# Order of small steps and column ranges in a fused sparse linear, GELU and FP8 linear kernel

## Chip, cores and metric

The kernel runs on one core of a Trainium2 chip. The metric is the device time of one execution in microseconds (us), lower is better.

## What is computed

x has 4096 rows (8 x 512) of 1024 numbers. Every row is normalised, and two linear layers are applied to the result and added to x:

```
xn   = layernorm(x)                                    # per row, eps 1e-5
attn = (w1^T w2^T) * sparse_mask                        # 1024 x 1024, a band of stripes
y    = gelu(xn attn + b2)
w_q  = fp8_e4m3(weight * 448 / max|weight|)
x_q  = fp8_e5m2(xn * x_scale),  x_scale = 57344 / max|xn|     # one scale for the whole of xn
f    = (x_q w_q^T) / x_scale / w_scale + bias
out  = x + y + f
```

x_scale needs every row of x: no product with x_q can start before the last row is read, squared and searched for its maximum.

## The kernel before

The rows are 32 tiles of 128 (NT = 32), all of them kept in SBUF. Every engine has its program written out by hand in order; engines wait for each other with semaphores.

**First stage.** SyncE loads the weights and the tiles. ScalarE and VectorE make row sums (neg_mean). ScalarE's `square(t)` (L645) makes the squares with their sum (ssq) and counts `squared`; VectorE's `maximum(t)` (L868) takes each row's largest square. TensorE transposes the weights and multiplies w1 with w2; VectorE masks, scales and splits the result into a high and a low half (`attention_high` L906, `attention_low` L910). GpSimd rounds the weights, and makes from ssq, with `deviations(i)` (L534 scaled variance, L537 power -1/2, L540 product), the 1/deviation rs and -mean/deviation nb of the tiles of one entry of `RANGES`.

**The scale of x.** After the last square ScalarE makes var_all from ssq (L733). VectorE, in this order: maximum(31), L973 to L976 (x_rowmax), TensorE spreads it over the partitions, VectorE's L978 (x_sqmax), GpSimd's square root L597 (x_amax), VectorE's x_inv L1027 and x_mul L1028 (x_scale). Then VectorE does sum_parts(1) (L1013), add_b2(0) (L983), four small scalars (L1032 to L1036), add_b2(1), add_gelu(0), add_gelu(1) (L993), add_product(0) (L998), sum_parts(2), seed_f(2) (L1005), add_product(1), seed_f(3), sum_parts(3). GpSimd does `quantiser(0)` and `quantiser(1)` (L547, L548: rs and nb times x_mul, for the tiles of a range; each counts `quant_ready`), `add_bias(0)` and `add_bias(1)` (L578), the scaling of the bias (L605), low(4) and low(5).

**The tiles.** Tile q passes these steps:
- ScalarE `normalise(q)` (L739): x to xn * x_scale. It waits for `quant_ready` by the place of q's range in `RANGES` (`wait_range`, L330). `high(q)` (L745): its rounding to 16 bits.
- GpSimd `low(q)` (L553): what the rounding left.
- SyncE `transpose_parts(q)` (L419): a DMA that transposes both halves into hlT.
- GpSimd `quantise(q)` (L584): the sum of the halves as FP8. For tiles 1 to 3 it is VectorE's sum_parts(q) and ScalarE's quantise(q) (L754).
- TensorE `attention(a)` (L1195) for the pair a, a + 1 into psY and psZ, and `ffn(q)` (L1210) into psT or psF. attention(a) waits from tile 4 on for `seed_y` (L771) of both tiles, with which ScalarE puts b2 into PSUM.
- ScalarE `gelu(q)` (L761, from tile 4 on L765), VectorE `add_gelu(q)`, `add_product(q)`, and SyncE stores.

The engines' loops go over pairs, a = 0, 2, ... 30. TensorE: ffn(a), ffn(a + 1), attention(a + 2); before the loop attention(0), 6 warming matmuls, the spread and 8 more (L1228). ScalarE in turn a: gelu(a), gelu(a + 1) (for a > 0), normalise and high of a + 6, seed_y(a + 2), seed_y(a + 3), normalise and high of a + 7. GpSimd in turn a: low(a + 6), quantise(a + 4), low(a + 7), quantise(a + 5); at a = 2 and a = 8 also deviations and quantiser of the third and the fourth range. What waits on an engine holds up all that stands behind it on that engine.

Of the kernel before, what the change touches and what calls it, by code (L numbers as in the profile page):

```python
# [5 lines left out]
ALU = mybir.AluOpType  # L6
ACT = mybir.ActivationFunctionType
# [10 lines left out]
D = 1024  # L18
# [20 lines left out]
LN_EPS = 1e-5  # L39
AMAX_EPS = 1e-12  # L40
E4M3_MAX, E5M2_MAX = 448.0, 57344.0
XSCALE = 1024.0
# [10 lines left out]
NT = 32  # L53
# [1 line left out]
FIRST = 4  # L55
KEEP_WARM = (6, 8)

RANGES = [(0, 4), (4, 12), (12, 20), (20, 32)]
PAIRS = range(0, NT, 2)
SPREAD_AT = 20  # L60

# [35 lines left out]
def sparse_linear_plus_fp8_linear(  # L97
# [18 lines left out]
    with ExitStack() as ctx:  # L116
        def sb(name, shape, dt):
            return ctx.enter_context(nc.sbuf_tensor(name, shape, dt))
# [4 lines left out]
        def sem(name):  # L123
            return ctx.enter_context(nc.semaphore(name))
# [47 lines left out]
        ssq = sb("ssq", [P, NT], F32)  # L172
# [5 lines left out]
        var_all = sb("var_all", [P, NT], F32)  # L178
# [39 lines left out]
        biases_loaded = sem("biases_loaded")  # L218
# [24 lines left out]
        squared = sem("squared")  # L243
# [4 lines left out]
        var_all_ready = sem("var_all_ready")  # L248
# [81 lines left out]
        def wait_range(eng, signal, q):  # L330

            eng.wait_ge(signal, next(i for i, (lo, hi) in enumerate(RANGES) if q < hi) + 1)

        def wait_xs(eng, q):

            eng.wait_ge(first_xs if q < FIRST else xs_ready, q + 1 if q < FIRST else q - FIRST + 1)

        def wait_hlT(eng, q):

            eng.wait_ge(hlT_loaded[q % HLT_RING], 16 * (q // HLT_RING + 1))  # L340
# [5 lines left out]
        def wait_y(eng, q):  # L346

            for r, n in last_turns(q):
                eng.wait_ge(strip_done[r], n)
# [159 lines left out]
        def _(pool):  # L509
# [21 lines left out]
            def deviations(i):  # L531
                lo, hi = RANGES[i]
                pool.wait_ge(squared, hi)
                nc.gpsimd.tensor_scalar(var_s[:, lo:hi], ssq[:, lo:hi], 1.0 / D / XSCALE ** 2,  # L534
                                        LN_EPS / XSCALE ** 2, ALU.mult, ALU.add).then_inc(var_ready, 1)
                pool.wait_ge(var_ready, i + 1)
                nc.gpsimd.tensor_tensor(rs[:, lo:hi], var_s[:, lo:hi], minus_half[:, 0:hi - lo], ALU.pow)\  # L537
                    .then_inc(rs_ready, 1)
                pool.wait_ge(rs_ready, i + 1)
                nc.gpsimd.tensor_tensor(nb[:, lo:hi], neg_mean[:, lo:hi], rs[:, lo:hi], ALU.mult)\  # L540
                    .then_inc(nb_ready, 1)

            def quantiser(i):

                lo, hi = RANGES[i]
                pool.wait_ge(nb_ready, i + 1)
                nc.gpsimd.tensor_scalar(rs_q[:, lo:hi], rs[:, lo:hi], x_mul, None, ALU.mult)  # L547
                nc.gpsimd.tensor_scalar(nb_q[:, lo:hi], nb[:, lo:hi], x_mul, None, ALU.mult)\  # L548
                    .then_inc(quant_ready, 1)

            def low(q):
                wait_xs(pool, q)
                nc.gpsimd.tensor_tensor(hl[q % HL_RING][:, D:2 * D], xs[:, q % 2, :], hl[q % HL_RING][:, 0:D],  # L553
                                        ALU.subtract).then_inc(xl_ready, 1)

            def parts(q):
                x_q = x_all[:, SLOT[q], :]
                if q < HL_RING:
                    pool.wait_ge(a_step, KB)
                else:  # L560
                    wait_hlT(pool, q - HL_RING)
                nc.gpsimd.tensor_scalar(hl[q % HL_RING][:, 0:D], x_q, rs[:, q:q + 1], nb[:, q:q + 1],
                                        ALU.mult, ALU.add).then_inc(first_high, 1)
                if q == 2:
                    pool.wait_ge(x0_transposed, 1)
                nc.gpsimd.tensor_scalar(xs[:, q % 2, :], x_q, rs[:, q:q + 1], nb[:, q:q + 1],
                                        ALU.mult, ALU.add).then_inc(first_xs, 1)
                pool.wait_ge(first_high, q + 1)
                low(q)
# [4 lines left out]
            def add_bias(q):  # L574

                pool.wait_ge(biases_loaded, 32)
                wait_xs(pool, q)
                nc.gpsimd.tensor_tensor(x_all[:, SLOT[q], :], x_all[:, SLOT[q], :], bias_bc, ALU.add)\  # L578
                    .then_inc(bias_added, 1)

            def quantise(q):
                wait_hlT(pool, q)
                pool.wait_ge(f_done, q - XQ_RING + 1)
                nc.gpsimd.tensor_tensor(quantised(q % XQ_RING), hlT[:, q % HLT_RING, 0:D],  # L584
                                        hlT[:, q % HLT_RING, D:2 * D], ALU.add, saturate=False)\
                    .then_inc(xq_ready, 1)
# [6 lines left out]
            pool.wait_ge(xl_ready, 2)  # L593
            parts(2)
            parts(3)
            pool.wait_ge(x_sqmax, 1)
            nc.gpsimd.tensor_tensor(x_am, x_sq, plus_half[:, :], ALU.pow).then_inc(x_amax, 1)  # L597
            pool.wait_ge(x_scale, 1)
            quantiser(0)
            quantiser(1)  # L600
            add_bias(0)
            add_bias(1)
            pool.wait_ge(f_scale, 1)
            pool.wait_ge(bias_added, 2)
# [2 lines left out]
            def low_scaled(q):  # L607
                pool.wait_ge(xh_ready, q - FIRST + 1)
                low(q)
# [3 lines left out]
            for a in PAIRS:  # L613
                for q in (a, a + 1):
                    if q + AHEAD < NT:
                        low_scaled(q + AHEAD)
                    if q + FIRST < NT:
                        quantise(q + FIRST)
                if a in (2, 8):
                    deviations(2 + a // 8)  # L620
                    quantiser(2 + a // 8)

        @block.scalar
        def _(act):
# [10 lines left out]
            def square(t):  # L635
                wait_x(act, t)
                if KIND[t] == "A":
                    act.wait_ge(mean_a, sums_by("A", t))
                elif KIND[t] == "P":
                    act.wait_ge(mean_p, (sums_by("P", t) + 1) // 2)  # L640
                else:
                    act.wait_ge(mean_v, sums_by("V", t))
                if t >= SQ_RING:
                    act.wait_ge(row_max, t - SQ_RING + 1)
                act.activation(squares[:, t % SQ_RING, :], x_all[:, SLOT[t], :], ACT.Square,  # L645
                               bias=neg_mean[:, t:t + 1], accum_out=ssq[:, t:t + 1]).then_inc(squared, 1)
# [11 lines left out]
            def copy_wq(j):  # L658
# [70 lines left out]
            square(29)  # L729
            square(30)  # L730
            square(31)
            act.wait_ge(squared, NT)
            act.activation(var_all[:, :], ssq[:, :], ACT.Copy, scale=1.0 / D / XSCALE ** 2,  # L733
                           bias=LN_EPS / XSCALE ** 2).then_inc(var_all_ready, 1)

            def normalise(q):
                wait_range(act, quant_ready, q)
# [59 lines left out]
            with when_mask_leaves_band(act):  # L797
# [10 lines left out]
                with act.Fori(0, NT) as t:  # L808
                    act.wait_ge(g_x_loaded, 16 * t + 16)
                    act.activation(g_xs, x_slot, ACT.Identity, scale=rs[:, bass.ds(t, 1)],  # L810
                                   bias=nb[:, bass.ds(t, 1)]).then_inc(g_xs_ready, 1)
# [8 lines left out]
        def _(dve):  # L820
            chain = [0]

            def then(ins):

                chain[0] += 1
                ins.then_inc(v_chain, 1)
                dve.wait_ge(v_chain, chain[0])
# [38 lines left out]
            def maximum(t):  # L866
                dve.wait_ge(squared, t + 1)
                nc.vector.tensor_reduce(maxsq[:, t:t + 1], squares[:, t % SQ_RING, :], AX_X, ALU.max)\  # L868
                    .then_inc(row_max, 1)
# [98 lines left out]
            maximum(28)  # L968
            maximum(29)
            maximum(30)  # L970
            maximum(31)
            dve.wait_ge(var_all_ready, 1)
            then(nc.vector.reciprocal(m2[:, :], var_all[:, :]))  # L973
# [6 lines left out]
            def add_b2(q):  # L980
                wait_y(dve, q)
                y = ps_y[q % 2][:, :]
                nc.vector.scalar_tensor_tensor(out=y, in0=y, scalar=y_mul_first, in1=b2_bc, op0=ALU.mult,  # L983
                                               op1=ALU.add).then_inc(t1_ready, 1)
# [22 lines left out]
            def sum_parts(q):  # L1007
                wait_hlT(dve, q)
                if q == 1:
                    dve.wait_ge(wq_transposed, KB)  # L1010
                else:
                    dve.wait_ge(xq_first, q)
                nc.vector.tensor_tensor(xT, hlT[:, q, 0:D], hlT[:, q, D:2 * D], ALU.add).then_inc(xT_ready, 1)  # L1013

            def count_mask(b):
                if b < KB:
                    n = D - C1[b] + C0[b]
                else:
# [4 lines left out]
                nc.vector.tensor_scalar(buf[:, 0:n], buf[:, 0:n], 0.0, None, ALU.not_equal,  # L1023
                                        ALU.add, accum_out=cnt[:, b:b + 1]).then_inc(mask_counted, 1)

            dve.wait_ge(x_amax, 1)
            then(nc.vector.tensor_scalar(x_inv, x_am, XSCALE * AMAX_EPS, 1.0 / E5M2_MAX, ALU.max, ALU.mult))  # L1027
            nc.vector.reciprocal(x_mul, x_inv).then_inc(x_scale, 1)  # L1028
            sum_parts(1)
            dve.wait_ge(biases_loaded, 32)  # L1030
            add_b2(0)
            nc.vector.tensor_scalar(f_mul, x_inv, inv_ws, 1.0 / XSCALE, ALU.mult, ALU.mult)  # L1032
            nc.vector.tensor_scalar(y_mul, a_inv, x_inv, 1.0 / XSCALE, ALU.mult, ALU.mult).then_inc(y_scale, 1)
            dve.wait_ge(x_scale, 1)
# [272 lines left out]
```

## Time and profile before

| | us |
|---|---|
| median of 3 runs | 289.36 (289.15 to 291.16) |
| the profiled execution | 289.15 |
| its span | 287.4 |
| TensorE busy | 236.0 (82%) |
| VectorE busy | 218.4 (76%) |
| ScalarE busy | 202.0 (70%) |
| GpSimd busy | 193.1 (67%) |

The rows of the trace name engines PE (TensorE, matmuls), DVE (VectorE), ACT (ScalarE), POOL (GpSimd) and SPq (SyncE's DMA issues). Times are from the start of the span; L and a number is a line of the kernel. In timelines the brackets tell how long the engine sat idle before the instruction and what ended the idle time.

### The profile page before, as it was taken

The numbers are of one execution on the slowest core, as the hardware profiler recorded it, in microseconds if no ns is written. First come the engines' busy times: TensorE is split into PE (matmuls) and PEld (weight loads), VectorE is DVE, ScalarE is ACT, GpSimd is POOL, SyncE is SP. The second block draws the span as 40 slices with busy tenths as digits, with TensorE's granted clock in tenths as the row PEclk, the third lists the DMA queues.
The fourth block names the chain that finished last, engine by engine and source line by source line (L and its number), as shares of the span: only waits on it lengthen the run. The fifth ranks groups of instructions, "written<-read, shape, count | busy, mean of one in ns | idle before, by whom it ended". The sixth has DMA issues, their size and how long they took to land.

```text
span 287.4 us, 6791 instructions
## 1 busy us (share of the span) xinstructions
PE 236.0 (82%) x2745; PEld 163.0 (57%) x2745; DVE 218.4 (76%) x236; ACT 202.0 (70%) x242; POOL 193.1 (67%) x120
## 2 busy tenths in 40 slices
PE   0059799980446997369999999999999999999994
PEld 0049688870344363165756756747747657567561
DVE  3989989999997789576785785786877766766753
ACT  1099969999998555959678687696696696852320
POOL 2000699999995793899986997966967868754000
PEclk9999999996559799959999999999999999999998
DMA  7999999999998609889899899796796697785113
GB/s 284 418 411 410 407 409 408 409 382 409 329 238 144 189 2 138 230 205 221 221 241 209 242 207 216 229 232 149 218 196 165 188 166 212 182 190 180 73 78 146
DMA packets 83936, 68.84 MB, mean 240 GB/s; under 512 B 69696, under 2 KB 71488, under 8 KB 83904
## 3 DMA queue, kind: packets, MB, share of 16 engines
q1 hardware_dynamic: 83904, 68.40, 82.0%
q8 instruction: 22, 0.36, 0.5%
q14 instruction: 10, 0.08, 0.1%
HBM read 34.83 MB, written 16.78 MB: 180 GB/s over the span
## 4 chain that ended last, share of the span: by engine, by line
PE 60%; DVE 3%; ACT 2%; issue 2%; DMA 1%; POOL 1%; ACTq 0%; POOLq 0%; DVEq 0%
PE psT L1210 19%; PE psF L1210 18%; PE psY L1195 12%; PE psZ L1195 11%; DMA home<-home 1%; DVE maxsq L868 1%; PE psT L1228 1%; DVE wq_nat L1013 1%; POOL home L553 1%; ACT squares L645 0%; ACT home L739 0%; ACT junk L632 0%; ACT psZ L771 0%; DVE x_all L998 0%; ACT wqT L660 0%
## 5 line engine op out<-in xcount | busy, mean ns | idle before, releaser
L584 POOL TENSOR_TENSOR wq_nat<-home 128x1024 fp8e5<-128x1024 f16 x28 | 59.5, 2126 | 4.3 <-DMA home<-home 3.3
L553 POOL TENSOR_TENSOR home<-home 128x1024 f16<-128x1024 f32 x22 | 47.4, 2155 | 19.3 <-ACT home L745 18.8
L1210 PE MATMUL psF<-wqT,wq_nat 128*128 128x512 f16 x256 | 57.9, 379 | 1.6 <-ACT wq_nat L754 1.6
L1210 PE MATMUL psT<-wqT,wq_nat 128*128 128x512 f16 x256 | 58.2, 380 | 0.0
L1195 PE MATMUL psY<-split,home 64*128 64x200 f16 (+4 forms) x960 | 40.2, 233 | 11.8 <-ACT psZ L771 6.8
L765 ACT ACTIVATE psY<-psY,sc 128x1024 f32<-128x1024 f32 x14 | 15.2, 1088 | 46.8 <-PE psY L1195 46.8
L1195 PEld LDWEIGHTS psY<-split,home 64*128 64x128 f16 x960 | 37.3, 97 | 18.4 <-issue 18.4
L1210 PEld LDWEIGHTS psF<-wqT,wq_nat 128*128 128x128 fp8e5 x256 | 24.9, 98 | 32.1 <-ACT wq_nat L754 2.1
L993 DVE TENSOR_TENSOR x_all<-psY,x_all 128x1024 f32<-128x1024 f32 x16 | 19.6, 1224 | 30.4 <-ACT psY L765 26.6
L868 DVE TENSOR_REDUCE maxsq<-squares 128x1 f32<-128x1024 f32 x32 | 38.1, 1213 | 2.6 <-ACT squares L645 2.5
L1195 PE MATMUL psZ<-split,home 64*128 64x200 f16 (+4 forms) x960 | 40.0, 232 | 0.0
L1210 PEld LDWEIGHTS psT<-wqT,wq_nat 128*128 128x128 fp8e5 x256 | 23.9, 98 | 27.6 <-issue 0.7
L1195 PEld LDWEIGHTS psZ<-split,home 64*128 64x128 f16 x960 | 38.3, 96 | 0.0
L645 ACT ACTIVATE squares<-x_all,neg_mean 128x1024 f32<-128x1024 f32 x32 | 36.4, 1137 | 0.2
L739 ACT ACTIVATE home<-x_all,nb_q,rs_q 128x1024 f32<-128x1024 f32 x28 | 34.4, 1227 | 0.0
L998 DVE SCALAR_TENSOR_TENSOR x_all<-psT,sc,x_all 128x1024 f32<-128x1024 f32 x16 | 20.5, 1282 | 13.9 <-PE psT L1210 13.9
L632 ACT ACTIVATE junk<-x_all 128x1024 fp8e5<-128x1024 f32 x19 | 19.9, 1047 | 15.1 <-DMA x_all<-in_L_attn_x_dram 15.1
L553 POOL TENSOR_TENSOR hl<-home,hl 128x1024 f16<-128x1024 f32 x10 | 21.3, 2133 | 10.1 <-ACT hl L745 10.0
L524 POOL TENSOR_TENSOR x_all<-x_all,biases 128x1024 f32<-128x1024 f32 x4 | 8.5, 2136 | 28.9 <-DVE split L849 28.9
L998 DVE SCALAR_TENSOR_TENSOR x_all<-psF,sc,x_all 128x1024 f32<-128x1024 f32 (+1 forms) x17 | 20.7, 1220 | 5.4 <-PE psF L1210 5.3
L745 ACT ACTIVATE home<-home 128x1024 f16<-128x1024 f32 x19 | 20.1, 1057 | 0.6
L993 DVE TENSOR_TENSOR x_all<-psZ,x_all 128x1024 f32<-128x1024 f32 x16 | 19.4, 1214 | 1.1 <-POOL x_all L578 1.1
(112 smaller groups left out, 362.5 us busy)
## 6 DMA issues: line engine op xcount, KB each, us to landing
x_all<-in_L_attn_x_dram SPq DMA_DIRECT2D x32, 512.0 KB, 14.5
out_dram<-x_all SPq DMA_DIRECT2D x31, 512.0 KB, 3.3
x_all<-in_L_attn_w_dram SPq DMA_DIRECT2D x16, 512.0 KB, 15.4
x_all<-in_L_ffn_weight_dram SPq DMA_DIRECT2D x8, 512.0 KB, 6.4
squares<-_L_attn_sparse_mask_dram SPq DMA_DIRECT2D x2, 414.0 KB, 4.1
biases<-_L_attn_sparse_mask_dram SPq DMA_DIRECT2D x6, 132.0 KB, 10.7
squares<-_L_attn_sparse_mask_dram SPq DMA_DIRECT2D x2, 350.0 KB, 3.3
squares<-_L_attn_sparse_mask_dram SPq DMA_DIRECT2D x2, 286.0 KB, 3.2
```

Of the source, the lines that this page charges most:

```text
L553: nc.gpsimd.tensor_tensor(hl[q % HL_RING][:, D:2 * D], xs[:, q % 2, :], hl[q % HL_RING][:, 0:D], ALU.subtract).then_inc(xl_ready, 1)
L584: nc.gpsimd.tensor_tensor(quantised(q % XQ_RING), hlT[:, q % HLT_RING, 0:D], hlT[:, q % HLT_RING, D:2 * D], ALU.add, saturate=False)\
L632: act.activation(junk[:, n % 2, :], x_all[:, SLOT[t], :], ACT.Copy, scale=-1.0 / D, accum_out=neg_mean[:, t:t + 1], saturate=False).then_i ...
L645: act.activation(squares[:, t % SQ_RING, :], x_all[:, SLOT[t], :], ACT.Square, bias=neg_mean[:, t:t + 1], accum_out=ssq[:, t:t + 1]).then_ ...
L739: act.activation(xs[:, q % 2, :], x_all[:, SLOT[q], :], ACT.Identity, scale=rs_q[:, q:q + 1], bias=nb_q[:, q:q + 1]).then_inc(xs_ready, 1)
L745: act.activation(hl[q % HL_RING][:, 0:D], xs[:, q % 2, :], ACT.Copy).then_inc(xh_ready, 1)
L765: act.activation(y, y, ACT.Gelu, scale=y_mul).then_inc(gelu_ready, 1)
L868: nc.vector.tensor_reduce(maxsq[:, t:t + 1], squares[:, t % SQ_RING, :], AX_X, ALU.max)\
L993: nc.vector.tensor_tensor(x_q, ps_y[q % 2][:, :], x_q, ALU.add).then_inc(u_ready, 1)
L998: nc.vector.scalar_tensor_tensor(out=x_q, in0=ps_f[q % 2][:, cols], scalar=f_mul, in1=x_q, op0=ALU.mult, op1=ALU.add).then_inc(out_ready, 1)
L1195: ins = nc.tensor.matmul(ps_y[q % 2][:, lo:hi], hlT[rows, q % HLT_RING, part + P * b:part + P * b + P], A[rows, at:at + hi - lo], start=be ...
L1210: ins = nc.tensor.matmul(ps_f[q % 2][:, HALF * h:HALF * h + HALF], quantised(q % XQ_RING)[:, P * k:P * k + P], wqT[:, k, HALF * h:HALF * h ...
```

## The change

Four edits. The second range of `RANGES` ends at tile 8 and no longer at 12, and the third begins there: (4, 8) and (8, 20); GpSimd makes the third range at the end of turn a = 0 and the fourth at a = 10. GpSimd's add_bias(0) moves ahead of its wait for x_sqmax. VectorE's add_b2(0), with its wait for the biases, moves ahead of its wait for x_amax. var_all is made by VectorE between maximum(30) and maximum(31), not by ScalarE after square(31).

```diff
-RANGES = [(0, 4), (4, 12), (12, 20), (20, 32)]
+RANGES = [(0, 4), (4, 8), (8, 20), (20, 32)]
...
             parts(3)
+            add_bias(0)
             pool.wait_ge(x_sqmax, 1)
             nc.gpsimd.tensor_tensor(x_am, x_sq, plus_half[:, :], ALU.pow).then_inc(x_amax, 1)
             pool.wait_ge(x_scale, 1)
             quantiser(0)
             quantiser(1)
-            add_bias(0)
             add_bias(1)
...
-                if a in (2, 8):
-                    deviations(2 + a // 8)
-                    quantiser(2 + a // 8)
+                if a in (0, 10):
+                    deviations(2 + a // 10)
+                    quantiser(2 + a // 10)
...
             square(31)
-            act.wait_ge(squared, NT)
-            act.activation(var_all[:, :], ssq[:, :], ACT.Copy, scale=1.0 / D / XSCALE ** 2,
-                           bias=LN_EPS / XSCALE ** 2).then_inc(var_all_ready, 1)
...
             maximum(30)
+            dve.wait_ge(squared, NT)
+            nc.vector.tensor_scalar(var_all[:, :], ssq[:, :], 1.0 / D / XSCALE ** 2, LN_EPS / XSCALE ** 2,
+                                    ALU.mult, ALU.add).then_inc(var_all_ready, 1)
             maximum(31)
             dve.wait_ge(var_all_ready, 1)
...
+            dve.wait_ge(biases_loaded, 32)
+            add_b2(0)
             dve.wait_ge(x_amax, 1)
             then(nc.vector.tensor_scalar(x_inv, x_am, XSCALE * AMAX_EPS, 1.0 / E5M2_MAX, ALU.max, ALU.mult))
             nc.vector.reciprocal(x_mul, x_inv).then_inc(x_scale, 1)
             sum_parts(1)
-            dve.wait_ge(biases_loaded, 32)
-            add_b2(0)
             nc.vector.tensor_scalar(f_mul, x_inv, inv_ws, 1.0 / XSCALE, ALU.mult, ALU.mult)
```

## Rows read from the trace of the kernel before

**Rows 1.** Chain that ended last, in time: start, us, what, number of instructions
```profile
130.47 3.57 PE psT L1210 x16
...
141.68 3.58 PE psT L1210 x16
```

**Rows 2.** Timeline of PE, 94 to 125 us: start, us, instruction, count, idle before
```profile
94.01 3.49 PE L1228 MATMUL psT<-wqT,identH 128*128 128x512 f16 x8
97.29 3.75 PE L1210 MATMUL psT<-wqT,wq_nat 128*128 128x512 f16 x16
...
124.36 2.17 PE L1195 MATMUL psY<-split,home 64*128 64x132 f16 x30 [6.83 <-ACT psZ L771]
```

**Rows 3.** Timeline of ACT: quantise(0), quantise(3), normalise(8), seed_y(5)
```profile
95.56 1.11 ACT L754 ACTIVATE wq_nat<-psF,sc 128x1024 fp8e5<-128x1024 f32 x1 [3.45 <-DVE sc L1028]
...
112.70 1.15 ACT L754 ACTIVATE wq_nat<-wq_nat,sc 128x1024 fp8e5<-128x1024 f32 x1 [3.31 <-DVE wq_nat L1013]
...
120.03 1.23 ACT L739 ACTIVATE home<-x_all,nb_q,rs_q 128x1024 f32<-128x1024 f32 x1
...
123.20 1.01 ACT L771 ACTIVATE psZ<-biases 128x1024 f32<-128x1024 f32 x1
```

**Rows 4.** Timeline of POOL: low(5), low(6), and quantise(5), the last of turn 0
```profile
109.46 2.13 POOL L553 TENSOR_TENSOR hl<-home,hl 128x1024 f16<-128x1024 f32 x1 [1.48 <-ACT hl L745]
116.14 2.13 POOL L553 TENSOR_TENSOR home<-home 128x1024 f16<-128x1024 f32 x1 [4.56 <-ACT home L745]
...
122.40 2.12 POOL L584 TENSOR_TENSOR wq_nat<-home 128x1024 fp8e5<-128x1024 f16 x1
```

**Rows 5.** Timeline of POOL around the fourth range, 12 columns, at a = 8
```profile
162.72 2.12 POOL L584 TENSOR_TENSOR wq_nat<-home 128x1024 fp8e5<-128x1024 f16 x1
...
165.22 2.30 POOL L537 TENSOR_TENSOR rs<-var_s,minus_half 128x12 f32<-128x12 f32 x1
...
168.20 0.32 POOL L548 TENSOR_SCALAR nb_q<-nb,sc 128x12 f32<-128x12 f32 x1
```

**Rows 6.** Timeline of POOL: low(3), the root for x_amax, both add_bias
```profile
88.27 2.13 POOL L553 TENSOR_TENSOR home<-home 128x1024 f16<-128x1024 f32 x1
94.58 0.55 POOL L597 TENSOR_TENSOR sc<-sc,plus_half 128x1 f32<-128x1 f32 x1 [4.18 <-DVE sc L978]
...
97.67 4.66 POOL L578 TENSOR_TENSOR x_all<-x_all,biases 128x1024 f32<-128x1024 f32 x2
```

**Rows 7.** The bias: its issue, and from the DMA view KB and us to landing
```profile
81.54 0.44 SPq L452 DMA_DIRECT2D biases<-in_L_ffn_bias_dram  x1
...
biases<-in_L_ffn_bias_dram SPq DMA_DIRECT2D x1, 512.0 KB, 7.1
```

**Rows 8.** Timeline of DVE: maxima 29 to 31, x_inv, add_b2(0), add_gelu(1), sum_parts(3)
```profile
89.61 3.48 DVE L868 TENSOR_REDUCE maxsq<-squares 128x1 f32<-128x1024 f32 x3 [1.76 <-ACT squares L645]
...
95.17 0.15 DVE L1027 TENSOR_SCALAR sc<-sc 128x1 f32<-128x1 f32 x1 [0.67 <-POOL sc L597]
...
96.58 1.29 DVE L983 SCALAR_TENSOR_TENSOR psY<-psY,sc,biases 128x1024 f32<-128x1024 f32 x1
...
102.43 1.22 DVE L993 TENSOR_TENSOR x_all<-psZ,x_all 128x1024 f32<-128x1024 f32 x1 [1.09 <-POOL x_all L578]
...
109.54 3.12 DVE L1013 TENSOR_TENSOR wq_nat<-home 128x1024 f32<-128x1024 f16 x1
```

**Rows 9.** Timelines: low(1) on POOL, attention_high and the scaling of b2 on DVE
```profile
74.58 2.13 POOL L553 TENSOR_TENSOR home<-home 128x1024 f16<-128x1024 f32 x1
...
76.08 1.68 DVE L906 TENSOR_SCALAR split<-biases,sc 128x1976 f16<-128x1976 f32 x1
...
115.09 0.75 DVE L1054 TENSOR_SCALAR biases<-biases,sc 128x1024 f32<-128x1024 f32 x1
```

**Rows 10.** Windows: us, busy of PE, PEld, DVE, ACT, POOL, clock, DMA share, GB/s
```profile
124.30:128.30 4.00, 3.94 (x61) 3.98 (x63) 3.16 (x4) 2.13 (x2) 4.00 (x3) 0.50 1.09 265
```

## The prediction, made before the changed kernel was run

> **What bounds the kernel now.** I read the chain of work that ended last first, from its end backwards. From 130.47 us it is TensorE alone: a pair of token tiles costs 141.68 - 130.47 = 11.21 us, one pair like the next up to the last store [rows 1]. Nothing that the diff touches lies inside that loop, so a change can move the end only by moving the moment at which TensorE enters it for good. That moment is the start of attention(4) at 124.36, after 6.83 us of idle time that ScalarE ended [rows 2]. So the second view is ScalarE's timeline ahead of it: from quantise(3) at 112.70 it works without a gap through normalise and high of tiles 6 and 7, gelu(2) and gelu(3), then normalise(8) at 120.03, high(8), seed_y(4) and seed_y(5) at 123.20, which releases TensorE [rows 3]. From normalise(8) to TensorE's start it is 124.36 - 120.03 = 4.33 us. The reader should keep this order in mind: the two seeds stand behind normalise(8) on the same engine. The third view is what set 112.70: VectorE's sum_parts(3) (L1013), the releaser in its brackets; and what set that is, in the code, the row of small steps that makes the scale of x, after the last maximum.
>
> **Part 1: the table RANGES.** normalise(q) waits for as many quantisers as the range of q has as its place (wait_range). With (4, 12), tile 8 belongs to the second range, which GpSimd finishes before add_bias(0) at 97.67 [rows 6]. With (4, 8) it belongs to the third, (8, 20), and the third is now made at the end of a = 0 of GpSimd's loop, behind low(6), quantise(4), low(7) and quantise(5). Those four are 2.1 us each, back to back, the first at 116.14 and the last ending at 122.40 + 2.12 = 124.52 [rows 4]. Then come deviations(2) and quantiser(2) with 12 columns. The trace has that shape: from the end of the wide instruction ahead (162.72 + 2.12 = 164.84) to the end of the last small one (168.20 + 0.32 = 168.52) it is 3.68 us, 2.30 of it the power [rows 5]. On the times of before, normalise(8) would start at 124.52 + 3.68 = 128.20 in place of 120.03: 8.17 us late. Queued behind it on ScalarE are high(8), seed_y(4) and seed_y(5), and TensorE waits for the seeds with nothing else it may do, since its own work ahead of them is done 6.83 us earlier [rows 2]. So this part alone costs 8.2 us at the front of the loop, less what the rest brings GpSimd forward.
>
> What else it does is covered. deviations(1) has 4 columns and not 8, ahead of GpSimd's 4.18 us of idle time [rows 6]: nothing. The range (20, 32) moves from a = 8 to a = 10 with the same 12 columns, and tile 20 is first wanted at a = 14, two pairs or 22 us on: nothing. The old deviations(2) leaves a = 2, where GpSimd had to make room for it; that only gives slack behind the stall.
>
> **Part 2: add_bias(0) forward.** It stands now before GpSimd's wait for x_sqmax. low(3) ends at 88.27 + 2.13 = 90.40 [rows 6]. The bias was issued at 81.54 and took at most 7.1 us to land, 88.6 [rows 7], so it starts at 90.4, takes 4.66 / 2 = 2.33 us [rows 6] and ends at 92.73, inside the 4.18 us of idle time. Behind the scale it is gone: add_bias(1) ends 2.33 us earlier, and add_gelu(1), which sat 1.09 us idle for it [rows 8], moves along, and with it add_product(0), sum_parts(2), quantise(2), high(5), low(5), sum_parts(3).
>
> **Part 3: add_b2(0) forward on VectorE.** It was at 96.58, 1.29 us long, and it now stands ahead of x_inv, on which all of the above hangs. x_inv sat 0.67 us idle for GpSimd's root [rows 8]; that covers half. The scale comes 1.29 - 0.67 = 0.62 us later. TensorE doesn't feel it: the 8 warming matmuls run from 94.01 until ffn(0) at 97.29, while quantise(0), at 95.56, needs 1.11 us, so it has 0.6 us of room [rows 2, 3].
>
> **Part 4: var_all from ScalarE to VectorE,** between maximum(30) and maximum(31). As a small instruction it is 0.15 us (x_inv's size [rows 8] is the nearest; below nothing it cannot be, as in the old place ScalarE did it beside maximum(31)). But part 2 has put add_bias(0) beside it. What happens when a VectorE instruction of the form with one SBUF source meets a GpSimd one is in the trace: attention_high began at 76.08 while low(1) ran until 74.58 + 2.13 = 76.71, and took 1.68 us for 1976 elements, while an instruction of the same form with 1024 elements took 0.75 with GpSimd idle [rows 9]. Without the 76.71 - 76.08 = 0.63 us in which both ran, 1.05 us are left, which is what 0.75 us for 1024 let expect. sum_parts(3), an instruction with two SBUF sources, was started at 109.54, when low(5) (109.46 to 111.59) was running, and took 3.12 us, of which 111.59 - 109.54 = 2.05 lie beside low(5) [rows 4, 8]. So var_all, due at 89.61 + 3.48 x 2/3 = 91.93 [rows 8], may be held until add_bias(0) ends at 92.73: 0.80 + 0.1 = 0.9 us for the chain. The bounds are 0.15 and 0.95. I take 0.9, because attention_high is an instruction of this very form; only its width is another.
>
> The Trainium skill (SBUF — State Buffer, section "SBUF: two separate sides") says of the port pair that these two engines share that "whichever" of them "starts first gets the pair for the whole instruction; the other fully blocks". The trace agrees with it at sum_parts(3), 3.12 us. By that rule var_all is held and the sum is the one below; without it, it would be 0.75 us less.
>
> **The sum.** Front: + 0.9 (part 4) + 0.62 (part 3) - 2.33 (part 2) = -0.8 us for everything from add_bias(1) to quantise(5). quantise(5) ends at 124.52 - 0.8 = 123.7; + 3.68 = 127.4 is normalise(8), 7.35 us later than 120.03; + 4.33 = 131.7 is attention(4). Behind it GpSimd and ScalarE have the distances of before or better, so the 11.21 us a pair stay. The profiled execution took 289.15 us, 0.21 under the median of the runs shown: 289.15 + 7.35 = 296.5 us. If var_all isn't held: 6.6 us later, 295.75.
>
> **Rivals.**
> (a) The start is late, but the front is gained back once more. low(5) took the port at 109.46, just ahead of sum_parts(3) at 109.54. If the shifts of parts 2 to 4 turn that order round, sum_parts(3) ends its 2.05 us of waiting sooner and low(5) a little later, and low(6) with the rest of GpSimd's four comes 2.05 us sooner: + 5.3, 294.45 us, or 293.7 if var_all isn't held either. For it: the margin is 0.08 us. Against: both hang on sum_parts(2) through fixed instructions, so the margin should move along.
> (b) TensorE's clock. Before, it sat idle 6.83 us and then ran from 124.30 to 128.30 at a granted 0.50 of full speed, that is at 1.2 GHz [rows 10]; attention(4) took 130.47 - 124.36 = 6.1 us, where a pair of 11.21 us less two ffn of 3.5 leaves 4.2: 1.9 us lost to the low level. Now it is idle for some 15 us. Should the low level last twice as long, another 1.9 us are lost: 298.4 us.
> (c) The other side: not slower. The front gains and nothing pays: GpSimd would reach the third range before ScalarE's normalise(8) at 120.03 - 0.8. The point from which it decides: GpSimd's four wide instructions would have to end by 119.2 - 3.68 = 115.5 us, and the first of them starts at 116.14 - 0.8 = 115.3. The gain would then be the front's: 289.15 - 0.8 to - 1.6 = 287.5 to 288.4 us. Only if I misread the place of tile 8 in the table can it come out so.
> (d) The wait is there but half as long, because VectorE's or ScalarE's work of a = 0 is so reordered that quantise(4) or (5) falls behind deviations(2). Each of the two saves 2.1 us: 296.5 - 4.2 = 292.3 us with both. Against it is the code, in which the order on GpSimd is fixed; the chance is for something in its queue that I don't see.
>
> **How the numbers follow.** Forecast, 295.75 to 296.5, with less than a microsecond of small terms around it: 0.78. (a) 0.08, (b) 0.07, (c) 0.03, (d) 0.04. The range must hold (a) and most of (b): 293.7 to 298.3. A measurement of this kernel tells about 1%, 2.9 us, from no change. Slower by over 1% are the forecast, (a), (b) and half of (d): 0.95; within 1% (c) in most of its span and the rest of (d): 0.04; faster by over 1%: 0.01.
>
> **What would show it.** ScalarE's row of normalise(8) has idle time of 8 us ahead of it, ended by GpSimd's quantiser; the rows of the 12-column power stand at about 124.5 us and no longer behind a = 2; TensorE's idle time ahead of attention(4) grows from 6.8 to about 15 us; the distance of the pairs behind it stays 11.21 us. For the front: VectorE's first add_b2 ahead of x_inv, x_inv about 1.5 us later than 95.17, var_all 0.8 us or more long (held) or 0.2 (not); sum_parts(3) still about 3.1 us long. If normalise(8) doesn't wait, or waits for something other than the quantiser, I am wrong.

## The result, and the profile after

| | before | changed |
|---|---|---|
| median | 289.85 us (4 runs) | 298.24 us (4 runs, 297.15 to 298.75) |
| ratio | | 1.028, 95% interval 1.023 to 1.0328 |
| profiled execution | 289.15 us | 298.59 us |
| span | 287.4 us | 296.8 us |

The change costs 8.4 us by the medians. The two profiled executions lie further apart, 298.59 - 289.15 = 9.44 us, and the rows below have to account for those.

First the timeline of ScalarE in the changed kernel, gelu(3), normalise(8) and seed_y(5) (there L736 is normalise, L742 high, L768 seed_y, L865 maximum). They answer to [rows 3].

```profile
119.57 0.97 ACT L758 ACTIVATE psZ<-psZ 128x1024 f32<-128x1024 f32 x1
128.65 1.24 ACT L736 ACTIVATE home<-x_all,nb_q,rs_q 128x1024 f32<-128x1024 f32 x1 [8.11 <-POOL nb_q L548]
...
131.83 1.01 ACT L768 ACTIVATE psZ<-biases 128x1024 f32<-128x1024 f32 x1
```

8.11 us of idle time, ended by GpSimd's L548, the last instruction of quantiser(2). Before, the row had no brackets. Next GpSimd's timeline, which answers to [rows 4, 5, 6]: low(3), add_bias(0), low(6), quantise(5), the power with 12 columns and the end of quantiser(2).

```profile
89.61 2.13 POOL L553 TENSOR_TENSOR home<-home 128x1024 f16<-128x1024 f32 x1
91.70 2.34 POOL L578 TENSOR_TENSOR x_all<-x_all,biases 128x1024 f32<-128x1024 f32 x1
...
116.58 2.13 POOL L553 TENSOR_TENSOR home<-home 128x1024 f16<-128x1024 f32 x1 [4.56 <-ACT home L742]
...
122.83 2.12 POOL L584 TENSOR_TENSOR wq_nat<-home 128x1024 fp8e5<-128x1024 f16 x1
...
125.32 2.30 POOL L537 TENSOR_TENSOR rs<-var_s,minus_half 128x12 f32<-128x12 f32 x1
...
128.31 0.31 POOL L548 TENSOR_SCALAR nb_q<-nb,sc 128x12 f32<-128x12 f32 x1
```

From the start of low(6) to that of normalise(8) it is now 128.65 - 116.58 = 12.07 us and was 120.03 - 116.14 = 3.89 us: 8.18 us more. TensorE's timeline (against [rows 2]) shows who pays, and the chain in time (against [rows 1]) that nothing else does: the pairs still follow each other by 151.11 - 139.91 = 11.20 us.

```profile
96.23 3.62 PE L1228 MATMUL psT<-wqT,identH 128*128 128x512 f16 x8
99.65 4.30 PE L1210 MATMUL psT<-wqT,wq_nat 128*128 128x512 f16 x16
...
132.99 2.18 PE L1195 MATMUL psY<-split,home 64*128 64x132 f16 x30 [14.37 <-ACT psZ L768]
```

```profile
139.91 3.56 PE psT L1210 x16
...
151.11 3.58 PE psT L1210 x16
```

Last VectorE's timeline, against [rows 8]: maxima 29 and 30, var_all (L969), maximum(31), add_b2(0), x_inv, sum_parts(3).

```profile
90.19 2.35 DVE L865 TENSOR_REDUCE maxsq<-squares 128x1 f32<-128x1024 f32 x2 [0.99 <-ACT squares L645]
92.46 1.62 DVE L969 TENSOR_SCALAR var_all<-ssq 128x32 f32<-128x32 f32 x1
94.00 1.21 DVE L865 TENSOR_REDUCE maxsq<-squares 128x1 f32<-128x1024 f32 x1
...
96.69 1.28 DVE L983 SCALAR_TENSOR_TENSOR psY<-psY,sc,biases 128x1024 f32<-128x1024 f32 x1
97.88 0.15 DVE L1029 TENSOR_SCALAR sc<-sc 128x1 f32<-128x1 f32 x1
...
109.97 3.13 DVE L1013 TENSOR_TENSOR wq_nat<-home 128x1024 f32<-128x1024 f16 x1
```

An instruction over 32 columns takes 1.62 us: it ends at 94.08, and add_bias(0) on GpSimd ended at 91.70 + 2.34 = 94.04. The two share nothing in the code, and yet one sets the end of the other. This is what the text below calls holding: an instruction of one engine has started by its row, but ends only after the instruction that runs on the other. x_inv no longer has idle time ahead of it; add_b2(0) stands there now.

### The profile page after: what moved, and what is told of

It reads as the page before. It is cut to its first block, busy times and chain, and to the rows that moved or that the text cites. A ratio compares the mean times of both kernels' runs of the same rounds, so it can differ in the third digit from the quotient of the medians.

```text
span 296.8 us, 6791 instructions
## 1 busy us (share of the span) xinstructions
PE 236.7 (80%) x2745; PEld 163.4 (55%) x2745; DVE 221.0 (74%) x237; ACT 201.8 (68%) x241; POOL 193.8 (65%) x120
## 4 chain that ended last, share of the span: by engine, by line
PE 57%; DVE 4%; issue 4%; POOL 3%; ACT 2%; ACTq 0%; DVEq 0%; POOLq 0%
PE psT L1210 18%; PE psF L1210 16%; PE psY L1195 11%; PE psZ L1195 10%; DVE maxsq L865 1%; PE psT L1228 1%; DVE wq_nat L1013 1%; POOL home L553 1%; ACT home L736 1%; POOL rs L537 1%; POOL wq_nat L584 1%; DVE x_all L998 1%; DVE var_all L969 1%; DVE psT L1005 0%; ACT psY L768 0%
## 5 line engine op out<-in xcount | busy, mean ns | idle before, releaser
L1195 PE MATMUL psY<-split,home 64*128 64x200 f16 (+4 forms) x960 | 41.0, 235 | 19.3 <-ACT psZ L768 14.4
L1195 PEld LDWEIGHTS psY<-split,home 64*128 64x128 f16 x960 | 38.1, 98 | 26.0 <-issue 20.8
L736 ACT ACTIVATE home<-x_all,nb_q,rs_q 128x1024 f32<-128x1024 f32 x28 | 34.4, 1227 | 8.1 <-POOL nb_q L548 8.1
L865 DVE TENSOR_REDUCE maxsq<-squares 128x1 f32<-128x1024 f32 x32 | 38.1, 1212 | 1.7 <-ACT squares L645 1.6
L742 ACT ACTIVATE home<-home 128x1024 f16<-128x1024 f32 x19 | 20.1, 1057 | 0.6
L1005 DVE COPY psF<-biases 128x1024 f32<-128x1024 f32 x15 | 18.4, 1228 | 1.9 <-DVE x_all L998 0.5
```

The costliest lines, as they stand in the source:

```text
L736: act.activation(xs[:, q % 2, :], x_all[:, SLOT[q], :], ACT.Identity, scale=rs_q[:, q:q + 1], bias=nb_q[:, q:q + 1]).then_inc(xs_ready, 1)
L742: act.activation(hl[q % HL_RING][:, 0:D], xs[:, q % 2, :], ACT.Copy).then_inc(xh_ready, 1)
L1005: nc.vector.tensor_copy(ps_f[q % 2][:, :], bias_bc).then_inc(f_seeded, 1)
L1195: ins = nc.tensor.matmul(ps_y[q % 2][:, lo:hi], hlT[rows, q % HLT_RING, part + P * b:part + P * b + P], A[rows, at:at + hi - lo], start=be ...
```

## The experiments

Executions differ in how late the first stage ends, ahead of anything touched here: the last square, square(31), began at 90.61 in the profile before, at 91.19 in the changed kernel's and as late as 92.08 in another. So beside the ratio each kernel has a distance that leaves this out, from the start of the last square to the start of attention(4), read from its one profile. It was 124.36 - 90.61 = 33.75 us before and is 132.99 - 91.19 = 41.80 us in the changed kernel. The ratios are to the kernel before in the same series.

| kernel | ratio (95%) | last square to attention(4), us | attention(4) itself, us |
|---|---|---|---|
| before | | 33.75 | 6.05 |
| changed | 1.028 (1.023 to 1.0328) | 41.80 | 6.86 |
| RANGES alone | 1.0264 (1.0241 to 1.0287) | 41.93 | 5.84 |
| the three moves alone | 0.9989 (0.9975 to 1.0004) | 33.32 | 5.89 |
| changed, seeds first | 1.0072 (1.0047 to 1.0098) | 31.97 | 6.85 |
| changed, third range sooner | 1.019 (1.0164 to 1.0216) | 39.09 | 6.41 |
| add_bias(0) alone | 1.0023 (1.0 to 1.0046) | 34.02 | 6.18 |
| var_all alone | 1.0014 (0.9997 to 1.003) | 33.86 | 6.00 |
| add_bias(0) and add_b2(0) | 0.9935 (0.9915 to 0.9954) | 32.05 | 6.47 |
| add_bias(0) and var_all | 1.0046 (1.0024 to 1.0068) | 35.55 | 5.68 |
| seeds first alone | 0.9948 (0.9928 to 0.9967) | 32.36 | 6.27 |
| sum_parts(3) first alone | 0.9883 (0.9861 to 0.9904) | 30.81 | 6.72 |
| add_bias(0), add_b2(0), seeds | 0.9887 (0.9862 to 0.9912) | 30.32 | 6.36 |
| the same and sum_parts(3) first | 0.9697 (0.9672 to 0.9722) | 27.23 | 4.19 |

### RANGES alone

```diff
-RANGES = [(0, 4), (4, 12), (12, 20), (20, 32)]
+RANGES = [(0, 4), (4, 8), (8, 20), (20, 32)]
...
-                if a in (2, 8):
-                    deviations(2 + a // 8)
-                    quantiser(2 + a // 8)
+                if a in (0, 10):
+                    deviations(2 + a // 10)
+                    quantiser(2 + a // 10)
```

> Only the table RANGES and the turns at which GpSimd makes the ranges are changed; the three moves around the scale of x are left out. Theory A (the third range stands behind quantise(5) on GpSimd, and normalise(8) with both seeds waits for it): normalise(8) sits some 9 us idle for GpSimd, and the time is 8.2 us above the kernel before, ratio 1.028. If the three moves gained 0.8 us in the changed kernel, as predicted, this one is 0.8 us slower than it, ratio 1.031. Rival B (the moves cost something, and part of the 8.4 us is theirs): ratio 1.025 or less.

298.04 us. The timelines of ScalarE and TensorE of this kernel:

```profile
129.46 1.24 ACT L739 ACTIVATE home<-x_all,nb_q,rs_q 128x1024 f32<-128x1024 f32 x1 [8.13 <-POOL nb_q L548]
...
133.79 2.18 PE L1195 MATMUL psY<-split,home 64*128 64x132 f16 x30 [15.05 <-ACT psZ L771]
```

41.93 - 33.75 = 8.18 us, the whole of the loss, and what the 4 wide instructions and the 3.68 us of small ones give (8.17 us; that the two agree to 0.01 us is chance, as the distance of var_all alone, a kernel no slower than before, is already 0.11 us off). The ratio lies between theory A's 1.028 and rival B's 1.025, and its interval holds both. It doesn't hold 1.031, the figure for moves that gain 0.8 us in the changed kernel; whether they gain less or cost something this run doesn't tell. The next one takes them by themselves.

### The three moves alone

The changed kernel with RANGES and GpSimd's turns as they were.

> The three moves (add_bias(0), add_b2(0), var_all) with the old RANGES. As predicted: 0.8 us faster than before, ratio 0.997, no idle time ahead of normalise(8). Rival B, from the changed kernel's profile, where var_all was held 1.5 us and ffn(0) began 2.4 us later: attention(4) starts no sooner than before against the end of the last square, ratio 0.999 to 1.003.

289.60 us: the ratio is rival B's 0.999, and its interval just leaves out the predicted 0.997. The distance is 0.43 us shorter, half of the 0.8 predicted, nothing that the times tell from no change. The timelines of GpSimd and VectorE:

```profile
90.83 2.35 POOL L578 TENSOR_TENSOR x_all<-x_all,biases 128x1024 f32<-128x1024 f32 x1
...
91.92 1.30 DVE L969 TENSOR_SCALAR var_all<-ssq 128x32 f32<-128x32 f32 x1
```

add_bias(0) ends at 93.18, var_all at 93.22.

### Two doses of the wait

Both kernels are the changed one with one thing more. In the first, ScalarE seeds before it normalises in turn a = 2; in the second, GpSimd makes the third range ahead of quantise(5).

```diff
+                if a == 2:
+                    seed_y(4)
+                    seed_y(5)
                 if a + AHEAD < NT:
                     normalise(a + AHEAD)
                     high(a + AHEAD)
                 for q in (a + 2, a + 3):
-                    if FIRST <= q < NT:
+                    if FIRST + 2 <= q < NT:
                         seed_y(q)
```

> The changed kernel, but ScalarE does seed_y(4) and seed_y(5) before normalise(8). normalise(8) still waits for the third range until about 128 us. Theory A (the loss is only what is queued behind the waiting instruction): attention(4) starts at about 123.5 us and nearly the whole loss is gone, ratio to before 0.996 to 1.003. Rival C (tiles 8 and 9 being late is itself the loss, through their transposes): the stall moves to attention(6) or attention(8), ratio above 1.015.

292.23 us, between the two theories. attention(4) does start sooner than before the change (31.97 us against 33.75). The rest is in the timelines of ScalarE and TensorE:

```profile
128.58 1.24 ACT L736 ACTIVATE home<-x_all,nb_q,rs_q 128x1024 f32<-128x1024 f32 x1 [5.58 <-POOL nb_q L548]
...
133.04 1.07 ACT L762 ACTIVATE psY<-psY,sc 128x1024 f32<-128x1024 f32 x1
...
138.21 1.01 ACT L768 ACTIVATE psZ<-biases 128x1024 f32<-128x1024 f32 x1
...
139.36 1.21 PE L1198 MATMUL psY<-split,home 64*128 64x132 f16 x30 [2.28 <-ACT psZ L768]
```

ScalarE still stands at normalise(8) until 128.58, and now gelu(4) is behind it, which has no idle time ahead of it at 133.04: it came from the queue, not from TensorE. It hands on what the slack doesn't take, and seed_y(7), the last row but one, is late for attention(6), which sat idle 2.28 us for it. So theory A's queue was the right place, but seeing only the first victim in it was too little: the next pair's seeds stand there too. Rival C's transposes did not end that wait, TensorE's row names ScalarE.

```diff
+                    if q == 1:
+                        deviations(2)
+                        quantiser(2)
                     if q + FIRST < NT:
                         quantise(q + FIRST)
-                if a in (0, 10):
-                    deviations(2 + a // 10)
-                    quantiser(2 + a // 10)
+                if a == 10:
+                    deviations(3)
+                    quantiser(3)
```

> The changed kernel, but GpSimd makes the third range before quantise(5), not behind it. Theory A: normalise(8) starts one wide instruction, 2.1 us, sooner, idle time 6.0 us in place of 8.1, and the time is 2.1 us below the changed kernel's, ratio to before 1.020 to 1.022. If normalise(8) waited for something else than GpSimd's order (for low(7) or for a slow power alone), it doesn't move: ratio 1.028.

295.85 us, and ScalarE's timeline has the 6.0 us:

```profile
126.27 1.24 ACT L739 ACTIVATE home<-x_all,nb_q,rs_q 128x1024 f32<-128x1024 f32 x1 [6.05 <-POOL nb_q L548]
```

One wide instruction less ahead of the range, 2.06 us less idle time. GpSimd's order is the cause, and the price is counted in its instructions. The distance fell by more, 41.80 - 39.09 = 2.71 us: var_all was held for only 0.58 us in this execution and not for 1.62, and add_product(0) on VectorE sat 0.38 us idle for ffn(0), which it didn't in the changed kernel (2.06 + 1.04 - 0.38 = 2.72).

### What ate the gain of the front

Four kernels with the old RANGES take the three moves apart. The edits are the hunks of the change: add_bias(0) alone, add_bias(0) with add_b2(0), add_bias(0) with var_all, var_all alone.

> The kernel before with add_bias(0) alone moved ahead of the wait for x_sqmax. add_gelu(1) waited for add_bias(1) until 102.43 and would now wait for gelu(1), which ended at 100.72 and leaves the DVE chain free at about 101.3: 1.1 us sooner, attention(4) too. Ratio 0.996. If the wait for the bias was no term of the path: 1.000.

A miss: 1.0023, and 34.02 us where 33.75 - 1.1 = 32.65 was expected. The timelines of GpSimd (low(4)) and VectorE (sum_parts(2)):

```profile
103.73 2.13 POOL L553 TENSOR_TENSOR home<-home 128x1024 f16<-128x1024 f32 x1
...
103.78 3.16 DVE L1013 TENSOR_TENSOR wq_nat<-home 128x1024 f32<-128x1024 f16 x1
```

Before, sum_parts(2) started at 104.76 and took 1.21 us, and low(4) came 0.56 us after it, at 105.32, and waited (2.66 us for its 2.13). Counted from x_inv, low(4) comes 2.30 us sooner here and sum_parts(2) 1.69. That is enough to turn their order round, by 0.05 us, and sum_parts(2), which is on the path, sits out low(4): 1.95 us lost against 1.69 gained, the 0.27 us by which the distance has grown. This is what rival (a) of the prediction described for sum_parts(3), with the opposite sign and at the other instruction.

> add_bias(0) and add_b2(0) moved, var_all left on ScalarE and the old RANGES. If the holding of var_all by add_bias(0) is what ate the gain of the front: x_inv 0.6 us later and add_bias(1) 2.3 us sooner against it, 1.7 us in all, attention(4) 32.1 us after the start of the last square (33.75 before, 33.3 with all three moves), ratio 0.994. If the moves gain nothing anyway: the same as the three moves together, 0.999.

288.44 us, ratio and distance as expected (32.05 us). From x_inv (95.88 with add_bias(0) alone, 96.30 here) to low(4) it is 7.85 and 7.84 us, but to sum_parts(2) 7.90 and 7.29 us: with add_b2(0) out of VectorE's way sum_parts(2) is first again.

```profile
103.59 1.21 DVE L1013 TENSOR_TENSOR wq_nat<-home 128x1024 f32<-128x1024 f16 x1
...
104.14 2.66 POOL L553 TENSOR_TENSOR home<-home 128x1024 f16<-128x1024 f32 x1
```

add_b2(0)'s move costs the scale 0.4 us and pays here by keeping the order. So with var_all left alone the two other moves gain 1.7 us, and with it 0.43: the third takes 33.32 - 32.05 = 1.27 us back.

> add_bias(0) and var_all moved, add_b2(0) where it was. Theory: var_all sits behind add_bias(0) and takes 1.2 to 1.6 us, so that x_inv comes that much later than with add_bias(0) alone; ratio 1.000, against 0.996 for add_bias(0) alone. Rival: the long var_all is its own cost and not that of the neighbour, or is covered by maximum(31): 0.996.

> The kernel before with var_all alone moved to VectorE. GpSimd does nothing at that time. If the 1.3 to 1.6 us of var_all were waiting for add_bias(0), it is 0.2 us long here and the time is within 0.15 us of before, ratio 1.0005; if they are its own, it is as long as there and the ratio 1.004.

With add_bias(0) beside it var_all took 1.48 us (add_bias(0) ended at 93.42, var_all at 93.46), and the distance rose by 35.55 - 34.02 = 1.53 us over add_bias(0) alone. The absolute ratio expected, 1.000, stood on add_bias(0) gaining, which it doesn't alone; the step from one to the other, 0.0023, is less than the 0.004 expected, but their intervals overlap and the second has attention(4) 0.5 us shorter. In this kernel too sum_parts(2) came after low(4), by 0.06 us, and took 3.15 us. With nothing beside it VectorE's timeline shows:

```profile
92.65 0.18 DVE L969 TENSOR_SCALAR var_all<-ssq 128x32 f32<-128x32 f32 x1
```

0.18 us, and the time isn't to be told from before. The rest of the 0.58 to 1.62 us that it took in the five kernels with add_bias(0) beside it is waiting for the neighbour.

### Versions that beat both

> The kernel before, old RANGES, with seed_y(4) and seed_y(5) ahead of normalise(8) on ScalarE. They are free as soon as add_gelu(2) and (3) end, 120.5 and 121.6 us; attention(4) starts at about 122.8 in place of 124.4, and normalise(8) is 2 us later with slack to bear it: 1.6 us faster, ratio 0.9945. Rival: ScalarE's order is not the limit and the two us come back at attention(6) as they did with the late third range: 1.000.

288.58 us, and 1.39 us by the distance: nothing comes back at attention(6), since here normalise(8) has nothing to wait for.

The next one moves the instruction of [rows 8] that sat out low(5):

```diff
             add_product(1)
-            seed_f(3)
             sum_parts(3)
+            seed_f(3)
```

> The kernel before with VectorE's sum_parts(3) ahead of seed_f(3). It then starts at about 108.3, before low(5) at 109.5 has the port: 1.2 us long in place of 3.1, done 3.1 us sooner, and low(5) loses next to nothing. Theory: quantise(3) and all that follows it on ScalarE come 3 us sooner, attention(4) at 30.7 us after the start of the last square (33.75 before), ratio 0.989. Rival: seed_f(3) and add_b2(2), now later, or something else on GpSimd, take 2 us of it back: 0.996.

286.75 us, and VectorE's and GpSimd's timelines:

```profile
109.83 1.22 DVE L1013 TENSOR_TENSOR wq_nat<-home 128x1024 f32<-128x1024 f16 x1
...
111.08 2.13 POOL L553 TENSOR_TENSOR hl<-home,hl 128x1024 f16<-128x1024 f32 x1 [1.48 <-ACT hl L745]
```

2.94 us by the distance: 3.12 - 1.22 = 1.9 us of holding, and about 1.1 for seed_f(3), which no longer stands ahead. low(5) starts 0.03 us after sum_parts(3) has ended and loses nothing. Both together with the good two of the three moves:

> The same without the move of sum_parts(3): add_bias(0), add_b2(0) and the seeds. 1.8 + 1.5 us sooner if they add up, attention(4) 30.5 us after the start of the last square, ratio 0.988.

> Old RANGES, var_all on ScalarE, and four moves together: add_bias(0), add_b2(0), the two seeds ahead of normalise(8), sum_parts(3) ahead of seed_f(3). If they add up (1.8 + 1.5 + 3.1 us) attention(4) starts 27.4 us after the start of the last square, ratio 0.978. If TensorE or a transpose becomes the limit: 0.983 or more.

286.88 and 281.27 us. The distances add up as expected (30.32 and 27.23 us). The last kernel's ratio was missed on the good side, 0.9697 for 0.978: it is 290.06 - 281.27 = 8.8 us faster than before, and the distance gives 33.75 - 27.23 = 6.5 of them. TensorE's timeline has 1.9 us more, in attention(4):

```profile
118.48 1.21 PE L1198 MATMUL psY<-split,home 64*128 64x132 f16 x30 [2.16 <-ACT psZ L771]
```

And this stretch over attention(4) shows the clock (columns as in [rows 10]):

```profile
118.50:122.70 4.20, 4.20 (x121) 4.18 (x122) 4.02 (x5) 4.14 (x4) 4.20 (x3) 1.00 1.07 207
```

After 2.16 us of idle time attention(4) starts with matmuls at little over half the duration of [rows 2] (1.21 us for 30, against 2.17) and takes 4.19 us in all, at a granted clock of 1.00. It took 5.68 to 6.86 us after 4.6 to 15 us of idle time in every other kernel here (6.05 before). So the low clock of [rows 10] was not entered. A short idle time doesn't assure that, though. With add_bias(0) and var_all, TensorE sat idle for 2.12 us ahead of ffn(3), as short as here, and the next 3.2 us ran at 0.50:

```profile
115.80 5.26 PE L1210 MATMUL psF<-wqT,wq_nat 128*128 128x512 f16 x16 [2.12 <-ACT wq_nat L751]
...
115.80:119.00 3.20, 3.20 (x8) 1.20 (x9) 1.91 (x2) 3.17 (x3) 0.95 (x1) 0.50 1.10 334
```

There ffn(3) took 5.26 us in place of 3.62. Ahead of ffn(3) with the seeds first alone it was 2.15 us, and nothing was lost (3.63 us). What decides between the two the runs don't show.

## Why the prediction was right, and where its sizes were off

The forecast was 7.35 us on the profiled execution of before, 296.5 us, in a likely band of 295.75 to 296.5. The median is 298.24: the mechanism came as foretold, and the time came out 1.7 us above that band, 0.06 us inside the end of the range. 0.7 us of this is where the sum began: 289.15 is the fastest of the four executions of before, whose median is 289.85. The other 1.04 us are the change itself, 8.4 us in place of 7.35. The upper end of the range was put there for rival (b), at 298.4 us, and by the number alone rival (b) would seem to have happened; as shown below it did so only in part, and the range held the result by luck as well. By its steps:

**Part 1, RANGES: right.** 8.17 us were predicted for the later start of normalise(8); it is 8.18 us in the changed kernel, counted from low(6), and 8.18 us by the distance with RANGES alone. Idle time of 8 us ahead of normalise(8), quantiser(2) as its releaser, 11.2 us a pair behind: as foretold.

**Part 2, add_bias(0): right here, incomplete alone.** It fits into GpSimd's idle time and comes off behind the scale: from x_inv to low(6) it was 116.14 - 95.17 = 20.97 us and is 116.58 - 97.88 = 18.70 us, 2.27 us less where 2.33 was put. What the working didn't have is that GpSimd's new lead can bring low(4) ahead of sum_parts(2), which then sits it out. In the changed kernel add_b2(0) prevents that, by luck of their sizes.

**Part 3, add_b2(0): right, a little too large.** x_inv follows the start of L978 by 97.88 - 96.48 = 1.40 us, where it was 95.17 - 94.21 = 0.96 before. That is 0.44 us later and not 0.62: the rows of successive instructions overlap by about 0.1 us each, and the working took the full duration of add_b2(0).

**Part 4, var_all: the mechanism right, the term mis-sized.** It was put at 0.9 us, with 0.95 as its upper bound, and took maximum(31) 94.00 - 92.46 = 1.54 us. The step that failed is "low(3) ends at 90.40, so add_bias(0) ends at 92.73": that came from one profile, and in this one GpSimd was 1.3 us later throughout the end of the first stage (low(3) at 89.61, not 88.27) while VectorE was 0.6 us later. How long var_all is held is the difference between the times of two engines, and that difference varies from execution to execution. In all five profiles with add_bias(0) beside it var_all starts 1.27 or 1.28 us after the last square does, and this is how far low(3), with add_bias(0) right behind it, is ahead:

| kernel | low(3) starts ahead of the last square, us | var_all takes, us | sum |
|---|---|---|---|
| changed | 1.58 | 1.62 | 3.20 |
| add_bias(0) and var_all | 1.72 | 1.48 | 3.20 |
| the three moves alone | 1.91 | 1.30 | 3.21 |
| changed, seeds first | 2.09 | 1.11 | 3.20 |
| changed, third range sooner | 2.62 | 0.58 | 3.20 |

The sum is the same throughout: the end of the neighbour sets the end of var_all. The changed kernel and the one with the third range sooner are the same program up to there, and have the smallest and the largest lead. The kernel before had 2.34 us, and the prediction reckoned with that one figure. The bound should have come from add_bias(0)'s full 2.3 us.

The evidence for the holding was read with a slip: 1.05 us for attention_high's 1976 elements is not what 0.75 us for 1024 lets expect, which is 1.45 us in proportion. The conclusion stands by other profiles. attention_high took between 1.42 and 2.90 us in the 14 kernels, and ended 1.04 to 1.06 us after low(1) in every one.

**The sum.** From the last square to low(6) it was 116.14 - 90.61 = 25.53 us and is 116.58 - 91.19 = 25.39 us: -0.14 in place of -0.8. With 0.58 us by which the last square itself began later in this execution, and 0.81 us by which attention(4) was longer (6.86 against 6.05), 7.35 + 0.66 + 0.58 + 0.81 = 9.4 us, which is what the profiled executions differ by. Of the 0.66, part 4 is 0.64, part 3 is -0.18 and part 2 is 0.06. The 0.14 us that are left are the matmul that spreads the maximum (L209), up to rounding: it took 0.47 us in place of 0.32, at a granted clock of 0.50 after 5.15 us of idle time, and VectorE sat 0.57 us idle for it ahead of L978, where it was 0.42. attention(4)'s excess of 0.81 us is the clock of rival (b), less than half of the 1.9 us that this rival put in. This window of the changed kernel (columns as in [rows 10]) has a mean of 0.54, so most of attention(4) ran at 1.2 GHz:

```profile
133.00:139.00 6.00, 6.00 (x100) 6.00 (x102) 0.00 (x0) 2.06 (x2) 6.00 (x4) 0.54 0.00 0
```

It isn't the price of the longer idle time, though: RANGES alone had 15.05 us of it and the shortest of these three attention(4), 5.84 us. Over all kernels that were idle for 4.6 to 15 us the figure moves between 5.7 and 6.9 us with no relation to the idle time.

**Rival (a)** did not happen at sum_parts(3), which is 3.13 us long in the changed kernel as it was; the order there is fixed by what follows sum_parts(2): low(5) starts 0.07 or 0.08 us ahead of sum_parts(3) in every kernel that leaves the latter in its place. **Rival (c)** is excluded by the 8.11 us, **(d)** by the order of GpSimd's rows.

## What to carry to other kernels

A range of small per-row figures is cheap wherever it is made, but the instruction that waits for it brings its whole engine queue along: before moving where such a range ends, find the first reader of every range and ask what stands behind that reader. And two instructions that share no data can still be one critical path. Here it happened between GpSimd's tensor_tensor with 1024 elements (low, add_bias) and two kinds on VectorE: a tensor_tensor with two SBUF sources (sum_parts), and a tensor_scalar from SBUF to SBUF with 32 columns or more (var_all, attention_high). Write down who starts first and by how much, since every shift on either engine, a gain too, can turn it round. Moving one such instruction by one place was worth more here (sum_parts(3), 1.2%) than the best pair of the moves at the front (0.65%).

## What the hardware showed that was not expected

The holding reaches down to small instructions. var_all reads 32 numbers a partition, 0.18 us by itself, and was held for as long as add_bias(0) ran, ending 0.04 us after it in the changed kernel, with the three moves alone and with add_bias(0) and var_all. The sentence of the Trainium skill that the prediction quotes (SBUF — State Buffer, section "SBUF: two separate sides") names no size either, and the trace agrees with it down to this one. It doesn't go down to a single column: before the change the first of the four small scalars, with one column, started on VectorE 0.11 us after add_bias(0) on GpSimd (97.67, [rows 6]) and was not held.

```profile
97.78 0.20 DVE L1032 TENSOR_SCALAR sc<-sc 128x1 f32<-128x1 f32 x1
```

Where between 1 and 32 columns the line runs, no run here shows.

The trace of before already had the holding of a small instruction, the other way round. These are deviations(0)'s and deviations(1)'s scaled variance on GpSimd:

```profile
65.72 0.20 POOL L534 TENSOR_SCALAR var_s<-ssq 128x4 f32<-128x4 f32 x1
...
76.80 1.01 POOL L534 TENSOR_SCALAR var_s<-ssq 128x8 f32<-128x8 f32 x1
```

The second ends at 77.81, 0.05 us after attention_high on VectorE (76.08 + 1.68 = 77.76, [rows 9]). With RANGES changed it has 4 columns, as the first has, and takes 1.01 us all the same.

One GpSimd instruction doesn't hold its neighbour as its row would have it. The scaling of the bias (L605) stands at 101.32 with 2.86 us in the kernel with add_bias(0) and add_b2(0), thus until 104.18, and sum_parts(2) started at 103.59 beside it and took its normal 1.21 us, while the next GpSimd instruction, low(4), was the one that waited. In the kernel before it is the same (L605 until 102.50 + 2.85 = 105.35, sum_parts(2) from 104.76, 1.21 us). Either this form stops holding before its row ends or the row is too long; the runs don't tell.
